# Another order of work on all five engines of an attention and feed-forward kernel, with four pieces of work on other engines

## The chip, the cores and the metric

The kernel runs on one core of one Trainium2 chip. The metric is the device time of one execution in microseconds. The core has five engines that each work through a queue of their own in order: TensorE (PE in the profile; PEld is its loading of weights), VectorE (DVE), ScalarE (ACT), GpSimd (POOL) and SyncE (SP), which here only issues DMA transfers.

## The reference

For each of 16 batch elements of 128 tokens by 256 features there is one attention layer with 32 heads of 8 features, whose keys and values come from a context of 128 tokens by 128 features, and one feed-forward layer of width 1024 with 4-bit rounding of weights and activations. Cut to what matters:

```python
q = layernorm(x) @ Wq ;  k, v = split(ctx @ Wkv)
q, k = rope(q, pos), rope(k, pos)
w = softmax(q k^T / sqrt(8))           # for each of 32 heads
x = x + (w v) @ Wout + bout
z = fake_quant(layernorm(x), s1, -8, 7)
h = z @ fake_quant(W1, max|W1|/7, -8, 7)^T + b1_q
h = fake_quant(relu(h), s2, 0, 15)
x = x + h @ fake_quant(W2, max|W2|/7, -8, 7)^T + b2_q
```

## The kernel before

One batch element b is the unit of work. Its way through the engines is:

- `project_qk` and `project_v` (TensorE), the rotation by `by_cosine` and `by_sine` (VectorE) and `rotate` (GpSimd), `transpose_rows` (TensorE). The result is split into a coarse part `T_hi` (`split_high`, ScalarE) and a rest `T_lo` (`split_low`, VectorE).
- SyncE stores both parts to the scratch tensor `scr` in DRAM and fetches them back in another layout, into `q_stack` and `k_stack`. There each head's 32 rows hold its features in both parts. The 128 partitions are four such row blocks, j = 0 to 3.
- The scores are computed twice, in four quarters u = 0 to 3. `scores_for_max(b, u)` writes `ps_max`, from bf16 halves, and VectorE's `maxima` reduces it. `transpose_maxima` and `copy_maxima` turn the maxima, and a DMA puts them into a spare row of `q_stack`. Then `scores_for_exp(b, u)` writes `ps_exp`, and ScalarE's `exponentials` reads it. `ps_max` and `ps_exp` exist once each, so quarter u waits until the reader of quarter u-1 is done.
- `weigh_values` (two halves), `copy_av`, `transpose_av`, `invert_sums` and `normalise`, `transpose_attn`, `copy_attnT`, `project_out`; then `residual`, `norm2_stats`, `norm2` (GpSimd), `round_x`, `clip_x`, `transpose_xq`, `copy_xqT`, `hidden` (two halves), `relu`, `clip_h`, `project_y`, `output`, `store`.

Which row blocks a quarter of scores uses is set by one line, the same in both score functions:

```python
j = 2 * (u % 2) + jj          # jj = 0, 1
rows = slice(32 * j, 32 * j + 32)
```

So quarters 0 and 2 use the row blocks 0 and 1, and quarters 1 and 3 use the row blocks 2 and 3.

The order on each engine is written out by hand as one loop over rounds s. `at(s - 3, work, u)` does the work for element b = s - 3 if there is one. The offset says how many rounds after the element's entry a step stands; the place in the list says what stands ahead of it in the round. The rounds of the different engines are counted apart. Elements enter one a round, so the last rounds hold only the late steps of the last elements.

Small matrix products share three PSUM banks, `ps_misc0` to `ps_misc2`. The table `BANK` says which piece uses which, and `claim` makes a piece wait until the reader of the piece ahead of it in the same bank is done.

Of the kernel before, what the change touches and what calls it, by code (L numbers as in the profile page):

```python
# [36 lines left out]
BANK = {"rows": 1, "y": 2, "xqT": 0, "h0": 0, "av": 1, "qk": 2, "attnT": 1, "h1": 1, "wo": 0, "w0": 1,  # L37
        "w1": 1, "v": 2, "mx": 0}
# [22 lines left out]
def xattn_ffn_kernel(nc, xin, pos, wq_d, wkv_d, wout_d, w1_d, w2_d, vecs_d, out_d):  # L61
    stack = ExitStack()
    with stack:
# [132 lines left out]
        wq_ready = sem("wq_ready")  # L196

# [51 lines left out]
        def _(sp):  # L249
# [82 lines left out]
            for s in range(BATCH + 8):  # L332
                if s == 5:
                    load_late()
                at(s - 4, fetch_keys, 1)
                at(s - 4, fetch_queries, 1)
                at(s - 5, place_maxima)
                if s == 4:
                    load_ffn(0)
                at(s - 3, store_q_hi)  # L340
                at(s - 8, store)
                at(s - 3, store_lo)
                at(s - 3, store_k_hi)
                if s == 4:
                    load_ffn(1)
                at(s, load_further)
                at(s - 3, fetch_queries, 0)
                at(s - 3, fetch_keys, 0)
            for r in range(2):
                sp.wait_ge(stored[r], 16 * BATCH // 2)  # L350

        @block.gpsimd
        def _(pool):
# [43 lines left out]

            pool.memset(ident[:, :], 0.0).then_inc(id_ready, 1)
# [7 lines left out]
            for s in range(BATCH + 5):  # L406
                at(s, norm)
                at(s - 3, residual_bias)
                at(s, rotate)
                at(s - 4, norm2)  # L410
                at(s - 5, output_bias)

        @block.scalar
        def _(act):
# [58 lines left out]
            for s in range(BATCH + 5):  # L473
                at(s - 3, exponentials, 1)
                at(s - 5, relu, 1)
                at(s - 3, exponentials, 2)
                at(s - 2, place_values)
                at(s - 3, exponentials, 3)
                at(s, split_high)
                at(s - 4, copy_xqT)  # L480
                at(s - 3, copy_av)
                at(s - 2, exponentials, 0)
                at(s - 4, relu, 0)
                at(s - 3, copy_attnT)

        @block.vector
        def _(dve):
# [45 lines left out]
            def fill_strips():  # L533


                dve.memset(v_strip[:, :, :, :, :], 0.0).then_inc(strips_ready, 1)
                dve.wait_ge(strips_ready, 1)
                for k in range(3):
                    dve.memset(v_strip[:, :, k::3, :, 9 * k + HD:9 * k + HD + 1], 1.0)
                dve.memset(v_strip[:, :, 7, :, 26:27], 1.0).then_inc(strips_ready, 1)  # L540

# [11 lines left out]
            def prepare_levels():  # L553
                dve.wait_ge(wmax_in_psum, 2)
                dve.tensor_copy(wmax_all[:, :], ps_misc[BANK["w1"]][:, 0:2]).then_inc(wmax_copied, 1)
                dve.wait_ge(wmax_copied, 1)
                link(dve.reciprocal(r_wmax[:, :], wmax_all[:, :]), wprep)
                link(dve.tensor_scalar(w_levels[:, :], r_wmax[:, :], QMAX, None, ALU.mult), wprep)
# [63 lines left out]

            def copy_maxima(b):
                need(dve, mx_in_psum, b + 1)
                if b >= 2:
                    dve.wait_ge(max_in[(b - 2) % STACKS], turn(b - 2, STACKS))
                dve.tensor_copy(mxT[:, b % 2, :], ps_misc[BANK["mx"]][0:HEADS, 0:128]).then_inc(mxT_ready, 1)
# [66 lines left out]
            for s in range(BATCH + 7):  # L694
                if s == 6:
                    quantise_weights(0)
                at(s - 7, output)
                at(s - 2, split_low)
                at(s - 3, maxima, 1)
                at(s - 5, invert_sums)  # L700
                if s == 4:
                    weight_maxima(1)
                at(s - 5, normalise)
                at(s, norm1_stats)
                at(s - 1, by_cosine)
                at(s - 3, maxima, 2)
                at(s - 1, by_sine)
                if s == 4:
                    spread_maxima()
                at(s - 5, residual)  # L710
                at(s - 3, maxima, 3)
                if s == 2:
                    fill_strips()
                at(s - 5, norm2_stats)
                if s == 5:
                    quantise_weights(1)
                if s == 4:
                    prepare_levels()
                if s == 3:
                    weight_maxima(0)  # L720
                at(s - 6, clip_h, 0)
                at(s - 6, clip_h, 1)
                at(s - 3, copy_maxima)
                if s == 4:
                    prepare_scales()
                    round_biases()
                at(s - 5, round_x)
                at(s - 5, clip_x)
                at(s - 2, maxima, 0)

        @block.tensor
        def _(pe):
# [164 lines left out]
            for s in range(BATCH + 6):  # L897
                at(s - 1, transpose_rows)
                at(s - 6, project_y)
                at(s - 5, transpose_xq)  # L900
                at(s - 4, weigh_values, 1)
                at(s - 2, scores_for_max, 1)
                at(s - 3, scores_for_exp, 0)
                at(s - 5, hidden, 0)
                at(s - 4, transpose_av)
                at(s, project_qk)
                at(s - 4, transpose_attn)
                at(s - 2, scores_for_max, 2)
                at(s - 3, scores_for_exp, 1)
                at(s - 5, hidden, 1)  # L910
                at(s - 4, project_out)
                if s == 3:
                    transpose_weight_maxima()
                at(s - 2, scores_for_max, 3)
                at(s - 3, scores_for_exp, 2)
                at(s - 3, weigh_values, 0)
                if s == 3:
                    spread_weight_maxima()
                at(s - 2, project_v)
                at(s - 2, transpose_maxima)  # L920
                at(s - 3, scores_for_exp, 3)
                at(s - 1, scores_for_max, 0)
# [47 lines left out]
```

## Time and profile before

| What | Value |
|---|---|
| Time, median of 3 runs | 241.31 us (241.07 to 246.26) |
| Time of the profiled execution | 240.79 us |
| Span of the profiled execution | 238.8 us |
| TensorE busy | 199.6 us (84%) |
| VectorE busy | 195.1 us (82%) |
| ScalarE busy | 149.3 us (63%) |
| GpSimd busy | 72.4 us (30%) |
| Mean granted TensorE clock | 0.897 of full |

The time is 2.0 us longer than the span. The span is what the trace covers. A share of busy time is a mean over the start, in which few elements are under way, the full middle, and the end.

### The profile page before, as it was taken

Reading aid. Unit: us, or ns where it says so; the run is one execution under the profiler, and the core shown is the slowest. Engines: PE = TensorE matmul, PEld = TensorE weight load, DVE = VectorE, ACT = ScalarE, POOL = GpSimd, SP = SyncE. Lnnn points to the kernel's source line nnn. Section 1 sums busy time; section 2 is a strip of 40 time slices with the busy share of each in tenths; the row PEclk is TensorE's granted clock in tenths of the full one; section 3 lists DMA queues with packets and bytes.
Section 4 is the critical chain, followed back from the end, with each engine's and each line's share of the span. In section 5 each row is a group of like instructions: output and inputs, shape, how many; then the busy total and the mean of one; then the engine's idle time right before and its main releaser. Section 6 shows DMA issues by size and latency. Waiting matters only on the chain.

```text
span 238.8 us, 7476 instructions
## 1 busy us (share of the span) xinstructions
PE 199.6 (84%) x2822; PEld 151.6 (63%) x2822; DVE 195.1 (82%) x394; ACT 149.3 (63%) x309; POOL 72.4 (30%) x121
## 2 busy tenths in 40 slices
PE   3453739799699999999999999899999987969653
PEld 2232416576478878878787878687877765757441
DVE  3555859979999999999999999999999979745241
ACT  4000004345487969787878788787979686878623
POOL 2432031402607162525334251607062303122030
PEclk9975555559899999999999999999999999999985
DMA  6358996519265848584856656685557362000000
GB/s 215 128 182 284 314 369 190 194 49 276 89 191 183 248 150 257 176 273 138 270 178 224 211 181 187 207 257 164 193 169 240 121 186 96 3 25 3 23 22 22
DMA packets 37234, 41.12 MB, mean 172 GB/s; under 512 B 2640, under 2 KB 34384, under 8 KB 36944
## 3 DMA queue, kind: packets, MB, share of 16 engines
q1 hardware_dynamic: 37056, 40.65, 53.0%
q8 instruction: 22, 0.36, 0.6%
q14 instruction: 12, 0.10, 0.2%
q10 hardware_dynamic: 144, 0.02, 0.0%
HBM read 25.19 MB, written 15.20 MB: 169 GB/s over the span
## 4 chain that ended last, share of the span: by engine, by line
PE 54%; issue 23%; DVE 8%; DMA 8%; POOL 4%; ACT 2%; ACTq 0%; POOLq 0%; DVEq 0%; SPq 0%
PE ps_misc L734 30%; PE ps_av L734 11%; PE ps_exp L734 7%; PE ps_max L734 6%; DMA q_stack<-scr 4%; DMA scr<-T_lo 2%; DVE mx L619 2%; POOL x_b L396 1%; DMA pos_sb<-in_fside_BxSx_dram 1%; POOL rot L375 1%; ACT h_i L464 1%; POOL x_b L382 1%; DVE wmax L544 1%; ACT T_hi L420 1%; DVE T_lo L611 1%
## 5 line engine op out<-in xcount | busy, mean ns | idle before, releaser
L619 DVE TENSOR_REDUCE mx<-ps_max 128x8 f32<-128x1024 f32 x64 | 77.8, 1216 | 8.4 <-PE ps_max L734 8.1
L436 ACT ACTIVATE expo<-ps_exp 128x1024 f32<-128x1024 f32 x64 | 65.8, 1028 | 15.6 <-PE ps_exp L734 14.1
L375 POOL TENSOR_TENSOR rot<-by_cos,by_sin 128x512 f32<-128x512 f32 x16 | 20.4, 1275 | 97.6 <-issue 92.2
L464 ACT ACTIVATE h_i<-ps_misc,b1q,relu_scale 128x128 int16<-128x128 f32 x128 | 47.8, 462 | 2.0 <-PE ps_misc L734 1.9
L734 PE MATMUL ps_exp<-q_stack,k_stack 32*128 32x128 f32 x512 | 44.8, 295 | 0.4 <-ACT expo L436 0.4
L734 PE MATMUL ps_max<-k_stack,q_stack 32*128 32x128 bf16 x512 | 28.0, 231 | 15.8 <-issue 8.2
L734 PEld LDWEIGHTS ps_exp<-q_stack,k_stack 32*128 32x128 f32 x512 | 35.5, 196 | 6.2 <-issue 5.1
L734 PE MATMUL ps_av<-expo,v_strip 128*32 128x128 f32 x1024 | 37.2, 289 | 0.1
L734 PEld LDWEIGHTS ps_max<-k_stack,q_stack 32*128 32x128 bf16 x512 | 16.3, 98 | 30.3 <-issue 15.4
L734 PEld LDWEIGHTS ps_av<-expo,v_strip 128*32 128x32 f32 x1024 | 27.7, 115 | 3.6 <-ACT expo L436 0.7
L734 PE MATMUL ps_misc<-wkv,x_in 128*128 128x256 f32 x64 | 24.1, 462 | 0.4 <-DMA wkv<-in_L_xattn_Wkv_dram 0.3
L420 ACT CAST T_hi<-ps_misc 128x512 fp32r<-128x512 f32 x16 | 9.3, 583 | 24.0 <-PE ps_misc L734 23.8
L388 POOL TENSOR_TENSOR rstd<-var,minus_half 128x1 f32<-128x1 f32 x16 | 10.3, 644 | 45.9 <-DVE var L661 45.9
L734 PE MATMUL ps_misc<-xqT,w1T 128*128 128x128 bf16 x256 | 20.6, 227 | 1.0 <-ACT xqT L454 0.6
L734 PE MATMUL ps_misc<-w2T,hq 128*128 128x256 bf16 x128 | 17.6, 281 | 3.2 <-DVE hq L680 3.2
L734 PE MATMUL ps_misc<-wq,x_in 128*128 128x256 f32 x64 | 20.0, 443 | 0.0
L734 PEld LDWEIGHTS ps_misc<-xqT,w1T 128*128 128x128 bf16 x256 | 15.2, 101 | 3.6 <-ACT attnT L448 0.7
L734 PE MATMUL ps_misc<-wout,attnT 128*128 128x256 f32 x64 | 17.4, 394 | 0.0
L430 ACT COPY v_strip<-ps_misc 128x96 f32<-128x96 f32 (+1 forms) x48 | 8.0, 244 | 14.9 <-PE ps_misc L734 14.9
L734 PEld LDWEIGHTS ps_misc<-wq,x_in 128*128 128x128 f32 x64 | 14.3, 226 | 2.9 <-DVE wq L530 0.4
L734 PEld LDWEIGHTS ps_misc<-w2T,hq 128*128 128x128 bf16 x128 | 12.3, 100 | 5.9 <-issue 3.5
L442 ACT COPY av<-ps_av 128x384 f32<-128x384 f32 x16 | 7.7, 478 | 12.4 <-PE ps_av L734 12.4
(93 smaller groups left out, 275.8 us busy)
## 6 DMA issues: line engine op xcount, KB each, us to landing
scr<-T_hi SPq DMA_DIRECT2D x32, 256.0 KB, 2.6
q_stack<-scr SPq DMA_DIRECT2D x32, 256.0 KB, 4.3
k_stack<-scr SPq DMA_DIRECT2D x32, 256.0 KB, 4.3
x_in<-in_xin_dram SPq DMA_DIRECT2D x16, 320.0 KB, 3.7
scr<-T_lo SPq DMA_DIRECT2D x16, 256.0 KB, 2.2
w<-in_L_ffn_W_dram SPq DMA_DIRECT2D x2, 1024.0 KB, 7.3
out_dram<-y SPq DMA_DIRECT2D x16, 128.0 KB, 1.7
scr<-pads SPq DMA_DIRECT2D x2, 256.0 KB, 4.3
```

Source lines behind the costliest of these rows:

```text
L375: pool.tensor_tensor(rot[:, b % 2, :], by_cos[:, :], by_sin[:, :], ALU.add).then_inc(rot_ready, 1)
L382: pool.tensor_tensor(x_b[:, b % 2, :], x_all[:, b, :], bout, ALU.add).then_inc(x_b_ready, 1)
L388: pool.tensor_tensor(rstd2[:, r, :], var2[:, r, :], minus_half[:, :], ALU.pow).then_inc(rstd2_ready, 1)
L396: pool.tensor_tensor(x2_b[:, r, :], x2[:, r, :], b2q[:, :], ALU.add).then_inc(x2_b_ready, 1)
L420: act.copy(T_hi[:, r, :, :].rearrange("p c e -> p (c e)"), ps_misc[BANK["rows"]][:, :]).then_inc(hi_ready, 1)
L430: ins = act.copy(v_strip[:, s, k::3, :, 9 * k:9 * k + HD], src[:, k::3, :, :])
L436: act.activation(expo[:, b % 2, u, :], ps_exp[:, :], ACT.Exp, scale=SCALE).then_inc(exp_done, 1)
L442: act.copy(av[:, r, :], ps_av[:, 0:384]).then_inc(av_copied, 1)
L464: ins = act.activation(h_i[:, r, f, :], ps_misc[BANK[("h0", "h1")[half]]][:, 128 * c:128 * c + 128], ACT.Relu, bias=b1q[:, f:f + 1], scale ...
L544: dve.tensor_reduce(out=wmax[:, n:n + 1], in_=w_flat[n], axis=AX.X, op=ALU.max, apply_absolute_value=True).then_inc(wmax_ready, 1)
L619: dve.tensor_reduce(out=out[:, 2 * (u % 2):2 * (u % 2) + 2, 4 * (u // 2):4 * (u // 2) + 4], in_=ps_max[:, :].rearrange("p (j g k) -> p j g ...
L734: return pe.matmul(out, lhsT, rhs, start=start, stop=stop, skip_group_check=True, **kw)
```

## The change

The loops of all five engines are written in another order and with other offsets. The loop of TensorE has BATCH + 8 rounds where it had BATCH + 6, that of VectorE BATCH + 10 (was BATCH + 7), that of SyncE BATCH + 11 (was BATCH + 8), that of GpSimd BATCH + 9 and that of ScalarE BATCH + 7 (both were BATCH + 5). The banks are shared out anew. Four pieces of work change their engine: the copy of the transposed maxima (`copy_maxima`) and the rounding of the two weight tensors (the first half of `quantise_weights`, now `round_weights`) go from VectorE to ScalarE, and `fill_strips` goes from VectorE to GpSimd, ahead of its loop. The clipping of the weights stays on VectorE as `clip_weights`.

```diff
-BANK = {"rows": 1, "y": 2, "xqT": 0, "h0": 0, "av": 1, "qk": 2, "attnT": 1, "h1": 1, "wo": 0, "w0": 1,
-        "w1": 1, "v": 2, "mx": 0}
+BANK = {"w0": 0, "wo": 0, "h1": 1, "w1": 2, "attnT": 2, "qk": 0, "v": 0, "rows": 1, "xqT": 2, "y": 0,
+        "mx": 0, "h0": 2, "av": 1}
...
+            def fill_strips():
+                pool.memset(v_strip[:, :, :, :, :], 0.0).then_inc(strips_ready, 1)
...
+            def round_weights(n):
+                act.wait_ge(levels_ready, 1)
+                act.activation(w_i[n][:, :], w_flat[n], ACT.Copy, scale=w_levels[:, n:n + 1]).then_inc(w_rounded[n], 1)
+
+            def copy_maxima(b):
+                need(act, mx_in_psum, b + 1)
+                if b >= 2:
+                    act.wait_ge(max_in[(b - 2) % STACKS], turn(b - 2, STACKS))
+                act.copy(mxT[:, b % 2, :], ps_misc[BANK["mx"]][0:HEADS, 0:128]).then_inc(mxT_ready, 1)
...
-            def quantise_weights(n):
-                link(dve.tensor_scalar(w_i[n][:, :], w_flat[n], w_levels[:, n:n + 1], None, ALU.mult), wprep)
+            def clip_weights(n):
+                dve.wait_ge(w_rounded[n], 1)
                 dve.tensor_scalar(w_q[n], w_i[n][:, :], QMIN, QMAX, ALU.max, ALU.min).then_inc(wq_ready, 1)
...
             column_means()
-            for s in range(BATCH + 6):
...
+            for s in range(BATCH + 8):
+                if s == 5:
+                    transpose_weight_maxima()
+                at(s - 7, project_out)
+                at(s - 2, scores_for_max, 1)
+                at(s - 4, scores_for_exp, 3)
+                at(s - 8, hidden, 1)
+                if s == 5:
+                    spread_weight_maxima()
+                at(s - 6, transpose_attn)
+                at(s, project_qk)
+                at(s - 4, weigh_values, 0)
+                at(s - 3, scores_for_exp, 0)
+                at(s - 2, scores_for_max, 2)
...
```

On TensorE the full rounds show it best. First the scores. `ps_exp` rows are a quarter of `scores_for_exp`, `ps_max` rows a quarter of `scores_for_max`; `wout` is `project_out`, `xqT,w1T` is `hidden`, `ident` with a tile is that tile's transpose, `wkv` and `wq` are `project_qk`. In a full round before, from `transpose_attn` on, with the quarters max 2, exp 1, then max 3, exp 2:

```order
L734 MATMUL ps_misc1<-ident,attn 128x128 x2
L734 MATMUL ps_max<-k_stack,q_stack 128x128 x8
L734 MATMUL ps_exp<-q_stack,k_stack 128x128 x8
L734 MATMUL ps_misc1<-xqT,w1T 128x128 x8
L734 MATMUL ps_misc0<-wout,attnT 128x256 x2
L734 MATMUL ps_max<-k_stack,q_stack 128x128 x8
L734 MATMUL ps_exp<-q_stack,k_stack 128x128 x8
L734 MATMUL ps_av<-expo,v_strip 32x128 x16
L734 MATMUL ps_misc2<-wkv,x_in 128x256
```

In a full round now, from `project_out` on, with the quarters max 1, exp 3, then exp 0, max 2:

```order
L743 MATMUL ps_misc0<-wout,attnT 128x256 x2
L743 MATMUL ps_max<-k_stack,q_stack 128x128 x8
L743 MATMUL ps_exp<-q_stack,k_stack 128x128 x8
L743 MATMUL ps_misc1<-xqT,w1T 128x128 x8
L743 MATMUL ps_misc2<-ident,attn 128x128 x2
L743 MATMUL ps_misc0<-wkv,x_in 128x256
L743 MATMUL ps_misc0<-wq,x_in 128x256 x2
L743 MATMUL ps_av<-expo,v_strip 32x128 x16
L743 MATMUL ps_exp<-q_stack,k_stack 128x128 x8
L743 MATMUL ps_max<-k_stack,q_stack 128x128 x8
```

Each `ps_max` row still stands beside a `ps_exp` row, but beside another quarter. The four neighbours of a round were (max 1, exp 0), (max 2, exp 1), (max 3, exp 2) and (exp 3, max 0). They are now (max 1, exp 3), (exp 0, max 2), (exp 1, max 3) and (exp 2, max 0).

Next the start of TensorE's queue, after the projection of elements 0 and 1. Before, the rows of element 1 (`ident,rot`) stand behind the first maxima scores of element 0:

```order
L734 MATMUL ps_misc1<-ident,rot 128x128 x4
L734 MATMUL ps_misc2<-wkv,x_in 128x256
L734 MATMUL ps_misc2<-wq,x_in 128x256 x2
L734 MATMUL ps_max<-k_stack,q_stack 128x128 x8
L734 MATMUL ps_misc1<-ident,rot 128x128 x4
L734 MATMUL ps_max<-k_stack,q_stack 128x128 x8
L734 MATMUL ps_misc2<-wkv,x_in 128x256
```

Now they stand ahead of them:

```order
L743 MATMUL ps_misc1<-ident,rot 128x128 x4
L743 MATMUL ps_misc0<-wkv,x_in 128x256
L743 MATMUL ps_misc0<-wq,x_in 128x256 x2
L743 MATMUL ps_misc0<-wkv,x_in 128x256
L743 MATMUL ps_misc1<-ident,rot 128x128 x4
L743 MATMUL ps_max<-k_stack,q_stack 128x128 x16
L743 MATMUL ps_misc0<-wkv,x_in 128x256
```

The rotated rows of element b moved from the round after `project_qk` into the same round, and its first maxima scores stayed in the round after, so that a round now lies between the two.

Last the end of TensorE's queue. Before, from the last but one `project_out` on, the last two elements' exponential scores and weighted values still stand between the steps of the feed-forward layer:

```order
L734 MATMUL ps_misc0<-wout,attnT 128x256 x2
L734 MATMUL ps_exp<-q_stack,k_stack 128x128 x8
L734 MATMUL ps_av<-expo,v_strip 32x128 x16
L734 MATMUL ps_exp<-q_stack,k_stack 128x128 x8
L734 MATMUL ps_misc2<-w2T,hq 128x256 x8
L734 MATMUL ps_misc0<-ident_bf,xq 128x128 x2
L734 MATMUL ps_av<-expo,v_strip 32x128 x16
L734 MATMUL ps_misc0<-xqT,w1T 128x128 x8
L734 MATMUL ps_misc1<-ident,av 128x128 x3
L734 MATMUL ps_misc1<-ident,attn 128x128 x2
L734 MATMUL ps_misc1<-xqT,w1T 128x128 x8
L734 MATMUL ps_misc0<-wout,attnT 128x256 x2
```

Now, from the `project_out` of element 13 on, nothing else is left for the last three elements:

```order
L743 MATMUL ps_misc0<-wout,attnT 128x256 x2
L743 MATMUL ps_misc1<-xqT,w1T 128x128 x8
L743 MATMUL ps_misc2<-ident,attn 128x128 x2
L743 MATMUL ps_misc2<-ident_bf,xq 128x128 x2
L743 MATMUL ps_misc0<-w2T,hq 128x256 x8
L743 MATMUL ps_misc2<-xqT,w1T 128x128 x8
L743 MATMUL ps_misc0<-wout,attnT 128x256 x2
L743 MATMUL ps_misc1<-xqT,w1T 128x128 x8
L743 MATMUL ps_misc2<-ident,attn 128x128 x2
L743 MATMUL ps_misc2<-ident_bf,xq 128x128 x2
L743 MATMUL ps_misc0<-w2T,hq 128x256 x8
```

Behind the last quarter of exponential scores there were 13 rows, and there are 26 now: `project_out`, `transpose_xq` and `hidden` of elements 13, 14 and 15 each have a round of their own behind it.

## Rows read from the trace of the kernel before

**Rows 1.** The page: busy time, TensorE's granted clock, the chain that ended last.

```profile
PE 199.6 (84%) x2822; PEld 151.6 (63%) x2822; DVE 195.1 (82%) x394; ACT 149.3 (63%) x309; POOL 72.4 (30%) x121
...
PEclk9975555559899999999999999999999999999985
...
PE 54%; issue 23%; DVE 8%; DMA 8%; POOL 4%; ACT 2%; ACTq 0%; POOLq 0%; DVEq 0%; SPq 0%
```

**Rows 2.** Windows: two full rounds; length, busy PE, PEld, DVE, ACT, POOL, then PEclk, DMA.

```profile
68.88:79.89 11.01, 11.01 (x176) 8.84 (x177) 10.76 (x23) 8.65 (x20) 4.40 (x7) 1.00 0.67 212
...
91.25:102.20 10.95, 10.95 (x177) 8.55 (x177) 10.70 (x23) 9.04 (x21) 4.39 (x7) 1.00 0.70 218
```

**Rows 3.** Timeline of TensorE at 2.4 GHz, scores issued together: start, length, operation.

```profile
166.87 0.23 PE L734 MATMUL ps_max<-k_stack,q_stack 32*128 32x128 bf16 x2
166.90 0.33 PE L734 MATMUL ps_exp<-q_stack,k_stack 32*128 32x128 f32 x2
...
167.49 0.62 PE L734 MATMUL ps_misc<-xqT,w1T 128*128 128x128 bf16 x8
```

**Rows 4.** The same view, scores that did not run together.

```profile
73.67 0.66 PE L734 MATMUL ps_exp<-q_stack,k_stack 32*128 32x128 f32 x8
74.26 0.41 PE L734 MATMUL ps_max<-k_stack,q_stack 32*128 32x128 bf16 x8
74.59 0.66 PE L734 MATMUL ps_misc<-ident,rot 128*128 128x128 f32 x4
```

**Rows 5.** The chain that ended last, in order of time: the trip through DRAM.

```profile
24.69 2.96 DMA scr<-T_lo
27.71 6.83 DMA q_stack<-scr
```

**Rows 6.** Timeline of TensorE: a fourth quarter's exponential scores, then the last element.

```profile
96.01 0.55 PE L734 MATMUL ps_exp<-q_stack,k_stack 32*128 32x128 f32 x6
...
218.66 0.66 PE L734 MATMUL ps_exp<-q_stack,k_stack 32*128 32x128 f32 x8 [0.35 <-ACT expo L436]
...
225.12 1.08 PE L734 MATMUL ps_misc<-wout,attnT 128*128 128x256 f32 x4
...
229.88 0.27 PE L734 MATMUL ps_misc<-ident_bf,xq 128*128 128x128 bf16 x2 [0.90 <-DVE xq L673]
230.70 1.87 PE L734 MATMUL ps_misc<-xqT,w1T 128*128 128x128 bf16 x16 [0.55 <-ACT xqT L454]
```

**Rows 7.** Timeline of VectorE: what follows the last output projection, and the end.

```profile
226.24 0.42 DVE L650 TENSOR_TENSOR x<-ps_misc,x_b 128x256 f32<-128x256 f32 x1 [2.60 <-PE ps_misc L734]
...
236.11 0.48 DVE L687 SCALAR_TENSOR_TENSOR y<-ps_misc,h_scale,x_b 128x256 f32<-128x256 f32 x1 [1.13 <-PE ps_misc L734]
```

**Rows 8.** Groups by line and shape: count, busy us, mean ns, idle time before.

```profile
L619 DVE TENSOR_REDUCE mx<-ps_max 128x8 f32<-128x1024 f32 x64 | 77.8, 1216 | 8.4 <-PE ps_max L734 8.1 <-issue 0.2
L436 ACT ACTIVATE expo<-ps_exp 128x1024 f32<-128x1024 f32 x64 | 65.8, 1028 | 15.6 <-PE ps_exp L734 14.1
...
L734 PE MATMUL ps_misc<-xqT,w1T 128*128 128x128 bf16 x256 | 20.6, 227 | 1.0 <-ACT xqT L454 0.6 <-ACT attnT L448 0.5
...
L734 PE MATMUL ps_misc<-wq,x_in 128*128 128x256 f32 x64 | 20.0, 443 | 0.0
L734 PE MATMUL ps_misc<-w2T,hq 128*128 128x256 bf16 x128 | 17.6, 281 | 3.2 <-DVE hq L680 3.2
L734 PE MATMUL ps_misc<-wout,attnT 128*128 128x256 f32 x64 | 17.4, 394 | 0.0
...
L627 DVE CAST mxT<-ps_misc 32x128 fp32r<-32x128 f32 x16 | 4.4, 272 | 0.7 <-PE ps_misc L734 0.7
L365 POOL TENSOR_SCALAR var<-mv 128x1 f32<-128x1 f32 x16 | 4.2, 261 | 5.6 <-DVE mv L589 5.6
...
L561 DVE TENSOR_SCALAR w_i<-w,w_levels 128x2048 int16<-128x2048 f32 x2 | 2.6, 1278 | 0.0
...
L403 POOL MEMSET pads<- 128x256 f32 x1 | 0.3, 311 | 0.0
```

More of the change, by code:

```diff
@@ L405, in _ @@
             pool.wait_ge(id_ready, 3)
-            for s in range(BATCH + 5):
+            fill_strips()
+            for s in range(BATCH + 9):
                 at(s, norm)
[L408 to L411, printed above, removed]
+                at(s - 8, norm2)
+                at(s - 9, output_bias)
+                at(s - 1, rotate)
+                at(s - 6, residual_bias)
         @block.scalar
@@ L693, in _ @@
             spread_tables()
[L694 to L724, printed above, removed]
+            for s in range(BATCH + 10):
+                at(s - 9, residual)
+                if s == 9:
+                    clip_weights(1)
+                at(s - 9, norm2_stats)
+                at(s - 4, maxima, 1)
+                if s == 8:
@@ new lines, in _ @@
+                at(s, norm1_stats)
+                at(s - 4, maxima, 3)
+                at(s - 10, output)
+                at(s - 2, split_low)
+                at(s - 3, maxima, 0)
+                if s == 4:
+                    weight_maxima(0)
+                if s == 6:
+                    spread_maxima()
+                at(s - 6, invert_sums)
+                if s == 6:
+                    prepare_levels()
+                at(s - 6, normalise)
+                if s == 5:
+                    weight_maxima(1)
@@ L896, in _ @@
             column_means()
-            for s in range(BATCH + 6):
-                at(s - 1, transpose_rows)
-                at(s - 6, project_y)
-                at(s - 5, transpose_xq)
-                at(s - 4, weigh_values, 1)
-                at(s - 2, scores_for_max, 1)
-                at(s - 3, scores_for_exp, 0)
-                at(s - 5, hidden, 0)
-                at(s - 4, transpose_av)
[L906 to L922, printed above, removed]
+            for s in range(BATCH + 8):
+                if s == 5:
+                    transpose_weight_maxima()
[3 more added lines that the diff above has]
+                at(s - 8, hidden, 1)
+                if s == 5:
+                    spread_weight_maxima()
[4 more added lines that the diff above has]
+                at(s - 2, scores_for_max, 2)
+                at(s - 4, weigh_values, 1)
+                at(s - 1, project_v)
+                at(s - 3, scores_for_exp, 1)
+                at(s - 2, scores_for_max, 3)
+                at(s, transpose_rows)
+                at(s - 7, transpose_xq)
+                at(s - 8, project_y)
+                at(s - 3, scores_for_exp, 2)
+                at(s - 1, scores_for_max, 0)
+                at(s - 2, transpose_maxima)
+                at(s - 7, hidden, 0)
+                at(s - 4, transpose_av)
 _INS = ['xin', 'fside_BxSx2_0', 'L0_xattn_Wq', 'L0_xattn_Wkv', 'L0_xattn_Wout', 'L0_ffn_W1', 'L0_ffn_W2', 'vecs']
```

74 lines of the change are left out of this document (39 added, 35 removed).

## Prediction

> **What bounds the kernel now.** I read the page first: TensorE is busy for 84% of the span and VectorE for 82%, and more than half of the chain that ended last is TensorE's own work [rows 1]. The strip of the granted clock gives the three stages: a start up to about 54 us, mostly at 1.2 GHz; a full middle at 2.4 GHz; an end. Then windows of two full rounds, from one `transpose_attn` to the next. They last 11.01 and 10.95 us; in them TensorE has no idle time that the view can show and VectorE is busy for 10.76 and 10.70 [rows 2]. So in the middle TensorE sets the pace, with VectorE 0.25 us behind. Whatever lengthens TensorE's round is paid every round; what only relieves VectorE is worth little. As a milestone I use the fourth quarter of the exponential scores, exp(b, 3): it starts at 96.01 us for element 4 and at 218.66 for element 15 [rows 6], which is 122.65 / 11 = 11.15 us per element, 0.2 more than TensorE's work. After the last one the kernel needs 238.8 - 218.66 = 20.1 us.
>
> **The score pairs.** This is the largest term. A quarter for the maxima and a quarter for the exponentials, issued one behind the other, took 166.87 to 167.49 = 0.62 us [rows 3], and the first exponential product began 0.03 us after the first of the maxima. Alone, an exponential quarter took 73.67 to 74.26 = 0.59, and a maxima quarter 74.26 to 74.59 = 0.33 [rows 4]. So in a pair the maxima quarter is all but free: 0.62 against 0.92. Every such pair before joins quarters on different row blocks: (max 1, exp 0) is blocks 2, 3 beside 0, 1, and so on. After the change all four pairs join quarters of the same parity, which means the same row blocks: (max 1, exp 3), (exp 0, max 2), (exp 1, max 3), (exp 2, max 0). No row before shows such a pair, so its price is bounded: 0.62 if nothing changes, 0.92 if the two just follow each other. I take 0.92, because exponential quarters show what happens within a block: eight products on two blocks took 0.59, and adding eight on the other two blocks added only 0.03, so it is the sequence within a block that costs. That is 4 x 0.30 = 1.20 us per round: 10.95 + 1.20 = **12.15 us** for a full round.
>
> The Trainium skill (TensorE: Matmul & The Clock Gate, Part 3, "The mechanism") says that a load of weights overlaps products in flight only when the row group differs; the trace agrees where it can, with 0.62 for a pair on different blocks, and by that rule the sum stays as it is. The same page (Part 2, "Step-by-step") also lets the load run ahead when it goes to the background weight buffer; by that the pair would cost less than 0.92, and this is the first rival below.
>
> **The other three engines in a full round.** VectorE loses `copy_maxima`, 272 ns [rows 8], and needs about 10.5 us of the 12.15. ScalarE gains it: 9.0 [rows 2] plus about 0.3. Neither is the bound any more. I followed the banks and the single `ps_max` and `ps_exp` through a round of the new order: a maxima quarter needs 1216 ns on VectorE [rows 8] and about 0.3 us of signalling, an exponential quarter 1028 ns on ScalarE and as much; the shortest distances between quarters on TensorE are about 2 us. `copy_maxima` now stands ahead of exp 2 on ScalarE and waits for `transpose_maxima`, which TensorE issues behind exp 2 and max 0; exp 2 is delayed by about 1 us, behind which exp 3 (2.5 us later) is still in time. So full rounds cost 12.15 and no more.
>
> **Work moved off VectorE once.** `fill_strips`: at 311 ns for 256 elements per partition [rows 8] GpSimd needs at most 12 x 0.311 = 3.7 us for 3072, and it sat idle for 5.6 us ahead of its first `var` [rows 8]. Hidden; if it were not, it costs at most 1 to 2 us there. VectorE did this while it waited for the first scores, so nothing is gained either. Rounding the weights: 2 x 1278 ns leave VectorE, 2 x about 2.06 us (twice 1028 for 1024 elements) enter ScalarE, between two exponential quarters. The levels now come from a chain TensorE, VectorE, TensorE, VectorE in TensorE's round 5. I count 1.3 us there. Before, the same work held TensorE for some 2 us, so this is no loss, included below.
>
> **The start.** Before, `T_lo` of element 1 is stored at 24.69 us and its trip through DRAM (2.96, then 6.83) [rows 5] stands within one round, between the transposed rows and the first maxima scores. Now a round lies between them, and the rows of element 1 no longer queue behind the maxima of element 0. Carried forward by hand with the old durations, `T_lo` of element 1 is ready 4 us earlier, but the four maxima quarters and the projections then take turns, with TensorE at 1.2 GHz as before, and exp(0, 3) starts at about 47 (48.5 before). TensorE's round 4 begins at 46.7. Rounds 4 to 6 lack `hidden`, `project_y`, `project_out` and small transposes: 20.6/16 + 17.6/16 + 17.4/16 = 3.5 [rows 8] (records of `hidden` overlap a little, which about pays for the small transposes), 12.15 - 3.5 = 8.65 at 2.4 GHz. Round 4 I put at 12.8 (half of it at 1.2 GHz, 1.5 of waits, because without `project_y` exp 2 comes too soon behind exp 1, and without `project_out` max 1 too soon behind max 0); round 5 at 11.5 with the weights, round 6 at 10.4, round 7 at 11.2. So round 8 begins at 92.6 and **exp(4, 3) at 94.0**, 2 us earlier than before. Bounds: 86 with no waits, 100 with as many again.
>
> **The middle.** Rounds 8 to 15: 8 x 12.15 = 97.2, to 191.2. Rounds 16 to 18 lack more and more steps of the front (`project_qk`, `transpose_rows`, `project_v`, the maxima): I get 10.3, 9.4 and 8.3. exp(15, 3) starts at 219.2, against 218.66 before.
>
> **The end.** Before, `project_out` of elements 13 and 14 were done beside the scores of element 15. Now TensorE does them in rounds 20 to 22, one after another, with nothing else to do. Each is a chain: from `project_out` to `transpose_xq` 229.88 - 225.12 = 4.76 us, through VectorE and GpSimd [rows 6, 7]; then 0.2 for that transpose, 1.0 for `project_y`, 0.5 for a half of `hidden`; 6.5 in all, and TensorE works for 3.5 of them. The next `project_out` stands behind it in the queue. So: the rest of round 19, 5.3; rounds 20 and 21, 13.0; round 22 up to `hidden` 6.0; and from `hidden` of the last element to the end 238.8 - 230.70 = 8.1 [rows 6]. Together **32.4 us where it was 20.1**. Bounds: 5 and 9 us a round in place of 6.5, so 28 to 40.
>
> **The sum.** 219.2 + 32.4 = 251.6 us of span. Against 238.8: start -2.0; eight full rounds 8 x (12.15 - 11.15) = +8.0; rounds 16 to 18, 28.0 - 33.5 = -5.5; end +12.3; together +12.8. The profiled execution took 2.0 more than its span, and its 240.79 is 0.5 under the median of 241.31, so I forecast **254.1 us**.
>
> **Rivals.** (1) The pairs are still free or half free. The products would overlap although they share blocks. For it: within a quarter, each of the four turns on a block takes 0.59 / 4 = 0.15 us, and some of that may be loading that another product can hide. Against it: the 0.59 and 0.33 add up when apart. Price: about 55 pairs, 0.30 each, is 16.5 us: 254.1 - 16.5 = 237.6 if free, 246 if half. (2) On the other side, the start. The trip through DRAM held TensorE in every early round, and now it does not. If TensorE runs rounds 4 to 7 on its work alone, with the pairs free too (7.45 instead of 8.65 a round), exp(4, 3) comes at 82 to 83; then 8 x 10.95 + 25.9 + 32.4 gives 228 to 229 of span, 231 in time. It decides itself at round 4: only if exp(4, 3) starts ahead of about 88 can the kernel be faster by over 2%. Against it: `ps_max` and `ps_exp` exist once, and VectorE and ScalarE need 1.5 us and 1.4 us between quarters whatever the order. (3) The clock falls in the end. It went back to 1.2 GHz at about 231 before, after TensorE had worked little; rounds 20 to 22 are half empty. At 1.2 GHz `project_out`, `project_y` and `hidden` add about 2.5 us a round: 254.1 + 7.5 = 261.6. The same price would come from a start that is 6 us later.
>
> **How the numbers follow.** The forecast's case (248 to 258) gets 0.62; half-free pairs (241 to 248) 0.12; free pairs (235 to 241) 0.12; the clock or a later start (258 to 266) 0.10; the fast start 0.04. The range 241 to 262 leaves out most of free pairs, the fast start and the top of the slow case, two in ten. 2% is about what a measurement of this kernel can tell from no change: 236.5 to 246.1. Above it lie the forecast, the slow case and a part of half-free pairs, 0.77; within it 0.18; below it 0.05.
>
> **What would show it.** In the profile of the changed kernel: the distance from a `ps_max` quarter through its `ps_exp` neighbour near 0.9 us and not 0.62; full rounds near 12.15 us with TensorE busy throughout and VectorE idle for over 1 us in each; exp(4, 3) near 94 and exp(15, 3) near 219; behind it 32 us with three `project_out` 6.5 us apart. The prediction is wrong if pairs stay at 0.62, if full rounds wait for VectorE or ScalarE (a wait of `scores_for_max` for `maxima` in every round), or if the last `project_out` follows exp(15, 3) within 15 us.

## The result and the profile after

The changed kernel took 248.99 us (median of 4 runs, 247.4 to 250.68), the kernel before it 241.78 us beside it (4 runs, 241.07 to 246.26). The ratio is 1.031, with an interval of 1.025 to 1.037: the change makes the kernel slower. Here and below, ratios leave out runs that are over 1.5% longer than the shortest of their kernel, while medians count every run. The profiled execution took 247.4 us with a span of 245.6, which is 6.8 more than before.

The page of the changed kernel: busy time, TensorE's granted clock, and the chain that ended last, to be laid beside [rows 1]. A digit of PEclk is the clock granted to TensorE in one of 40 slices, in tenths of full speed.

```profile
PE 208.4 (85%) x2822; PEld 161.0 (66%) x2822; DVE 190.0 (77%) x371; ACT 152.2 (62%) x327; POOL 74.7 (30%) x126
...
PEclk9855757589958999999999999999999999997797
...
PE 51%; issue 23%; DMA 10%; DVE 6%; POOL 6%; ACT 2%; SPq 1%; ACTq 0%; POOLq 0%; DVEq 0%
```

TensorE has the same 2822 matmuls and is busy for 8.8 us more. The work is the same, so it got dearer where it stands. VectorE is 5 us less busy, and that bought nothing.

Windows of the changed kernel: a full round from `transpose_attn` to `transpose_attn`, and 2 us ahead of the full rounds (length, busy PE, PEld, DVE, ACT, POOL, then PEclk and DMA).

```profile
94.19:105.64 11.45, 11.45 (x180) 9.22 (x177) 10.79 (x22) 8.89 (x21) 4.42 (x7) 1.00 0.64 191
70.00:72.00 2.00, 2.00 (x14) 1.79 (x13) 1.90 (x6) 2.00 (x2) 0.00 (x0) 0.50 0.83 202
```

A full round is 11.45 us long where it was 11.01 and 10.95 [rows 2]. TensorE has no idle time in it, and VectorE is idle for 0.66. The second row is a loss that I hadn't looked for: at 2.4 GHz TensorE had just had three short waits, and then its clock was 1.2 GHz (granted 0.50) while TensorE, VectorE and ScalarE were full.

Timeline of TensorE after (start, length, operation, idle before), at two pairs of quarters in one full round and then the fourth quarter of element 15.

```profile
96.81 0.66 PE L743 MATMUL ps_exp<-q_stack,k_stack 32*128 32x128 f32 x8
97.32 0.40 PE L743 MATMUL ps_max<-k_stack,q_stack 32*128 32x128 bf16 x8
97.65 1.08 PE L743 MATMUL ps_av<-expo,v_strip 128*32 128x128 f32 x32
...
104.39 0.40 PE L743 MATMUL ps_max<-k_stack,q_stack 32*128 32x128 bf16 x8
104.61 0.64 PE L743 MATMUL ps_exp<-q_stack,k_stack 32*128 32x128 f32 x8
105.18 0.51 PE L743 MATMUL ps_misc<-xqT,w1T 128*128 128x128 bf16 x6
...
211.47 0.66 PE L743 MATMUL ps_exp<-q_stack,k_stack 32*128 32x128 f32 x8
...
216.99 1.09 PE L743 MATMUL ps_misc<-wout,attnT 128*128 128x256 f32 x4
...
221.75 0.27 PE L743 MATMUL ps_misc<-ident_bf,xq 128*128 128x128 bf16 x2 [2.77 <-DVE xq L685]
...
224.18 1.75 PE L743 MATMUL ps_misc<-wout,attnT 128*128 128x256 f32 x4
...
229.43 0.37 PE L743 MATMUL ps_misc<-ident_bf,xq 128*128 128x128 bf16 x2 [2.82 <-DVE xq L685]
...
232.16 1.18 PE L743 MATMUL ps_misc<-wout,attnT 128*128 128x256 f32 x4
...
237.00 0.27 PE L743 MATMUL ps_misc<-ident_bf,xq 128*128 128x128 bf16 x2 [3.22 <-DVE xq L685]
```

The two quarters of a pair now stand one behind the other in the trace, and no longer begin together as in [rows 3]. From start to start the pair takes 96.81 to 97.65 = 0.84 us with the exponentials first, and 104.39 to 105.18 = 0.79 with the maxima first, against 0.62. In the eight full rounds from 96.81 us on all 32 pairs take 0.78 to 0.84. The last three `project_out` begin at 216.99, 224.18 and 232.16. In each of these rounds TensorE waits about 3 us for `xq`, the end of the chain from the output projection through VectorE and GpSimd. Before there was one such round behind the scores [rows 6].

In three pieces, with exp(4, 3) at 93.16 and exp(15, 3) at 211.47, against the milestones of before [rows 6]: the start is 96.01 - 93.16 = 2.85 us shorter. The middle is 118.31 where it was 122.65, 4.3 shorter. What follows the last score is 245.6 - 211.47 = 34.1 where it was 20.1, 14.0 longer. The sum is +6.8. The middle is shorter in spite of longer full rounds. From exp(4, 3) to exp(12, 3) it takes 91.6 us where it took 89.5; from there to exp(15, 3) 26.7 where it took 33.2, since its last rounds have lost the feed-forward steps of the late elements. Those steps reappear in the end.

The kernel before didn't reach the 10.95 us of its best round in every round: the mean of those eight is 11.19. The pair of exp 3 and max 0 is the part of the round that varies. Timeline of TensorE before:

```profile
129.33 0.66 PE L734 MATMUL ps_exp<-q_stack,k_stack 32*128 32x128 f32 x8
130.47 0.40 PE L734 MATMUL ps_max<-k_stack,q_stack 32*128 32x128 bf16 x8 [0.48 <-issue]
```

In the nine full rounds from 96 to 186 us this fourth pair takes from 0.60 to 1.65 us, 1.04 in the mean, though it is on different row blocks; the other three take 0.61 or 0.62 each time. The view names no releaser. An estimate from the views of SyncE and of the tile puts it down to the trip through DRAM: the fetch of `k_stack` was issued at 125.74 and the median from issue to landing is 4.6, which is 130.3. In the new order a round lies between that trip and max 0.

### The profile page after: what moved, and what is told of

Its sections match the earlier page's. It is cut to its first block, busy times and chain, and to the rows that moved or that the text cites. A ratio compares the mean times of both kernels' runs of the same rounds, so it can differ in the third digit from the quotient of the medians.

```text
span 245.6 us, 7474 instructions
## 1 busy us (share of the span) xinstructions
PE 208.4 (85%) x2822; PEld 161.0 (66%) x2822; DVE 190.0 (77%) x371; ACT 152.2 (62%) x327; POOL 74.7 (30%) x126
## 4 chain that ended last, share of the span: by engine, by line
PE 51%; issue 23%; DMA 10%; DVE 6%; POOL 6%; ACT 2%; SPq 1%; ACTq 0%; POOLq 0%; DVEq 0%
PE ps_misc L743 27%; PE ps_exp L743 10%; PE ps_av L743 9%; PE ps_max L743 5%; DMA scr<-T_hi 4%; DMA w<-in_L_ffn_W_dram 4%; POOL x_b L384 2%; POOL x_b L398 2%; DVE mx L637 2%; DMA pos_sb<-in_fside_BxSx_dram 1%; DMA k_stack<-scr 1%; POOL rot L377 1%; ACT h_i L486 1%; ACT expo L448 1%; DVE by_sin L622 1%
## 5 line engine op out<-in xcount | busy, mean ns | idle before, releaser
L448 ACT ACTIVATE expo<-ps_exp 128x1024 f32<-128x1024 f32 x64 | 65.1, 1018 | 29.6 <-PE ps_exp L743 28.2
L743 PE MATMUL ps_av<-expo,v_strip 128*32 128x128 f32 x1024 | 35.2, 280 | 0.0
L390 POOL TENSOR_TENSOR rstd<-var,minus_half 128x1 f32<-128x1 f32 x16 | 8.9, 558 | 84.9 <-DVE var L673 84.9
L743 PEld LDWEIGHTS ps_av<-expo,v_strip 128*32 128x32 f32 x1024 | 26.7, 112 | 6.9 <-issue 5.0
L743 PE MATMUL ps_misc<-wkv,x_in 128*128 128x256 f32 x64 | 24.8, 474 | 3.5 <-DVE by_sin L622 3.3
L743 PE MATMUL ps_misc<-wq,x_in 128*128 128x256 f32 x64 | 21.0, 460 | 0.5 <-DVE wq L557 0.5
L743 PEld LDWEIGHTS ps_misc<-xqT,w1T 128*128 128x128 bf16 x256 | 16.7, 102 | 2.1 <-DVE attn L654 0.4
L743 PEld LDWEIGHTS ps_misc<-wkv,x_in 128*128 128x128 f32 x64 | 11.1, 217 | 8.4 <-DVE by_sin L622 4.3
L613 DVE TENSOR_TENSOR by_cos<-ps_misc,tabs 128x512 f32<-128x512 f32 x16 | 11.0, 690 | 7.0 <-PE ps_misc L743 6.0
L699 DVE SCALAR_TENSOR_TENSOR y<-ps_misc,h_scale,x_b 128x256 f32<-128x256 f32 x16 | 7.7, 483 | 11.1 <-PE ps_misc L743 11.1
```

What stands on the lines that cost most here:

```text
L390: pool.tensor_tensor(rstd2[:, r, :], var2[:, r, :], minus_half[:, :], ALU.pow).then_inc(rstd2_ready, 1)
L613: dve.tensor_tensor(by_cos[:, :].rearrange("p (c h d) -> p c h d", c=2, d=HD), ps_heads, bcast(tabs[:, b, :, 0:8], 2, HEADS), ALU.mult).th ...
L699: dve.scalar_tensor_tensor(out=y[:, r, :], in0=ps_misc[BANK["y"]][:, 0:DIM], scalar=h_scale[:, 1:2], in1=x2_b[:, r, :], op0=ALU.mult, op1= ...
L743: return pe.matmul(out, lhsT, rhs, start=start, stop=stop, skip_group_check=True, **kw)
```

## The experiments

Two causes were on record, the shared row blocks and the lengthened end. The first four kernels were made to take them apart, and to put them into the kernel before. All four ran on one chip and the later ones on others, each group beside the kernel before (241.26, 242.88 and 242.69 us), so across groups the ratios are surer than differences in us.

**Row blocks apart.** In the changed kernel only, the maxima quarters change parity, in the scores and in where `maxima` stores them. Each maxima quarter then stands beside an exponential quarter on the other two row blocks, in the same order of instructions.

```diff
-                out=out[:, 2 * (u % 2):2 * (u % 2) + 2, ...]
+                out=out[:, 2 * ((u + 1) % 2):2 * ((u + 1) % 2) + 2, ...]
...
-                        j = 2 * (u % 2) + jj
+                        j = 2 * ((u + 1) % 2) + jj
```

> The changed kernel with one thing undone: a quarter of the maxima scores now takes the other two row blocks (and the reduction writes the other columns), so that each of the four score pairs of a round joins quarters on different row blocks again, as in the kernel before. Order, banks and moved work stay as changed. Theory (pairs on shared blocks cost 0.79 to 0.84 us instead of 0.62): the round falls from 11.45 us to about 10.6, unless another engine takes over; with some 14 rounds under load this gives 8 to 11 us, so 237 to 240 us. Rival (the blocks do not matter and the round of 11.45 is due to waits of the new order): pairs keep 0.8 us and the time stays at 247 to 250.

It took 240.49 us (10 runs), ratio 0.994 to before (0.990 to 0.998), 8.5 us less than the changed kernel. Its full round:

```profile
101.25:112.00 10.75, 10.75 (x179) 8.59 (x177) 10.58 (x22) 8.71 (x21) 4.46 (x7) 1.00 0.72 216
```

Timeline of TensorE in that round, at one pair (start, length, operation).

```profile
103.88 0.33 PE L743 MATMUL ps_exp<-q_stack,k_stack 32*128 32x128 f32 x2
103.91 0.34 PE L743 MATMUL ps_max<-k_stack,q_stack 32*128 32x128 bf16 x6
...
104.47 1.08 PE L743 MATMUL ps_av<-expo,v_strip 128*32 128x128 f32 x32
```

In three of the four pairs the quarters begin together again, and this one is down to 104.47 - 103.88 = 0.59 us. The fourth, exp 2 and max 0, runs together only in part and takes 109.02 - 108.27 = 0.75; in other rounds it takes 0.64 to 0.75:

```profile
108.27 0.66 PE L743 MATMUL ps_exp<-q_stack,k_stack 32*128 32x128 f32 x8
108.68 0.41 PE L743 MATMUL ps_max<-k_stack,q_stack 32*128 32x128 bf16 x8
109.02 0.29 PE L743 MATMUL ps_misc<-ident,mx 128*32 128x128 f32 x1
```

The four pairs of this round take 2.54 us against 3.30 in the changed kernel's, which covers the 0.70 by which the round is shorter than 11.45. exp(4, 3) comes at 89.44, 3.7 us earlier than in the changed kernel, and exp(15, 3) at 201.78, 9.7 earlier. The end is as long as in the changed kernel, 236.5 - 201.78 = 34.7, so in the trace the row blocks leave the end alone.

**Row blocks shared.** The same edit in the kernel before, where it brings the pairs onto the same blocks.

> The kernel before with the same edit the other way round: its four score pairs now join quarters on the same row blocks, and nothing else is changed. Theory (shared blocks cost about 0.2 us a pair): the round grows from 10.95 to 11.75 us, 0.8 x 14 = 8 to 11 us more, so 249 to 253 us. Rival (the blocks do not matter): 241 to 242 us.

It took 245.87 us (4 runs), ratio 1.020 (1.012 to 1.028): slower than before, though by less than the 249 to 253 that I expected. The span is 242.4, 3.6 more than before. A full round and a pair in it:

```profile
104.05:115.45 11.40, 11.40 (x178) 9.35 (x178) 10.99 (x23) 8.97 (x21) 4.39 (x7) 1.00 0.58 182
```

```profile
104.37 0.40 PE L734 MATMUL ps_max<-k_stack,q_stack 32*128 32x128 bf16 x8
104.58 0.64 PE L734 MATMUL ps_exp<-q_stack,k_stack 32*128 32x128 f32 x8
105.15 0.62 PE L734 MATMUL ps_misc<-xqT,w1T 128*128 128x128 bf16 x8
```

The pair takes 0.78 us here too, so sharing is what makes it dear and not the new order. The round grew from 10.95 to 11.40, but the mean from exp(4, 3) to exp(15, 3) only from 11.15 to (222.62 - 97.76) / 11 = 11.35. The reason is the fourth pair, exp 3 and max 0. The three pairs with the maxima first went from 0.62 to 0.78 each, +0.5 us a round, but the fourth often stood apart already: its mean over nine full rounds was 1.04 before and is 0.89 here, so there was little overlap left for the shared blocks to take.

**One round less.** In the changed kernel everything from `transpose_attn` on stands one round earlier on all engines, and the weights' clipping, the scales and the late load with it. Only the offsets are touched.

```diff
-            for s in range(BATCH + 8):
+            for s in range(BATCH + 7):
...
-                at(s - 7, project_out)
+                at(s - 6, project_out)
```

> The changed kernel with everything from the transpose of the normalised attention on done one round earlier on all engines; the places within a round, the banks and the moved work stay. Theory (the end costs a round of its own for each late element, 6.5 to 8 us): one such round goes away, so 6 to 8 us less, 240 to 243 us, and the full rounds stay at 11.45. Rival 1 (the end is set by the clock, or by the chain of the last element alone): 247 to 250. Rival 2 (a round less of slack makes the full rounds wait for the normalisation): full rounds over 12 us, time 250 or more.

It took 242.75 us (10 runs), ratio 1.008 (1.003 to 1.012), 6.2 us less than the changed kernel. Rounds last 11.45 us as before the edit, exp(15, 3) comes at 213.67, and 240.6 - 213.67 = 26.9 us follow in place of 34.1. Two `project_out` are left behind the round of the last score, at 219.19 and 225.50. The end is 7.2 shorter; 2.2 of it went into the start, where exp(4, 3) now comes at 95.31 and not at 93.16. I put that down to the late steps entering its rounds sooner; it isn't shown.

**Both edits together.** Both mended, in the changed kernel.

> The changed kernel with both edits: different row blocks in each score pair, and the late steps one round earlier. If the two causes are separate, their gains add: 8 to 11 and 6 to 8 us off 249, so 230 to 235 us. If the start or VectorE is the bound without the shared blocks, less than the sum: 236 to 240.

It took 234.06 us (4 runs), ratio 0.972 (0.966 to 0.979). The two gains, 8.5 and 6.2, add up to 14.7, and both together gave 14.9. On this one chip, with the other edit in place each time, the row blocks are worth 242.75 - 234.06 = 8.7 us and the round 240.49 - 234.06 = 6.4. Rounds last 10.75, and 27.0 us follow the last score. The new order without its two costs is better than the old one.

**The strips later.** `fill_strips` moves behind the first three `norm` on GpSimd, out of the start.

```diff
-            fill_strips()
             for s in range(BATCH + 9):
                 at(s, norm)
+                if s == 2:
+                    fill_strips()
```

> The changed kernel with the filling of the value strips still on GpSimd, but in its round 2, where the trace shows 4 us of idle time, instead of ahead of its loop. Theory (GpSimd's fill from 1.93 to 4.59 us held VectorE's first copy, 0.98 us long instead of 0.18, and with it the whole start): the first copy takes 0.18 us again, every milestone of the start comes 0.9 us earlier, and the time falls by about 1 us, to 248. Rival (the longer first copy has to do with the late arrival of its input): the first copy stays at 0.98, no gain.

I made it because of these rows of the changed kernel. First VectorE at the start, then GpSimd (two calls of the same timeline):

```profile
3.65 0.98 DVE L525 COPY ang<-pos_sb 128x32 f32<-128x32 f32 x1 [2.67 <-DMA pos_sb<-in_fside_BxSx_dram]
3.74 0.91 DVE L526 TENSOR_SCALAR ang<-pos_sb 128x32 f32<-128x32 f32 x1
...
1.93 2.66 POOL L403 MEMSET v_strip<- 128x3072 f32 x1
...
8.48 0.24 POOL L367 TENSOR_SCALAR var<-mv 128x1 f32<-128x1 f32 x1 [3.54 <-DVE mv L607]
```

A copy of 32 elements took 0.98 us and ended at 4.63, 0.04 behind the end of the fill. GpSimd itself still waited 3.54 us ahead of its first `var`. With the strips filled later, in this kernel and in the one with all three edits alike, the same copy reads

```profile
3.61 0.18 DVE L526 COPY ang<-pos_sb 128x32 f32<-128x32 f32 x1 [2.63 <-DMA pos_sb<-in_fside_BxSx_dram]
```

So 0.8 us at the start is shown, and the first `var` of GpSimd comes at 7.78 and not at 8.48. The time was 248.73 us (4 runs, 245.88 to 259.3), ratio 1.019 (1.009 to 1.030) against 1.031 (1.025 to 1.037) for the changed kernel. The intervals overlap, so a gain in the total isn't shown. The profiled execution was the longest of the four; only its first microseconds are read here.

**The copy of the maxima back on VectorE**, behind `maxima(s - 3, 0)`; ScalarE loses it.

```diff
-                at(s - 2, copy_maxima)          # ScalarE
...
                 at(s - 3, maxima, 0)
+                at(s - 4, copy_maxima)          # VectorE
```

> The changed kernel with the copy of the transposed maxima back on VectorE, behind the reduction of the next element's first quarter. Theory (the forecast's: VectorE is not the bound, so where the copy runs is worth nothing by itself; but on VectorE it now stands behind a reduction of 1.22 us, and project_out waits for it through its bank): full rounds 0.3 to 0.5 us longer than 11.45, 4 to 6 us more in all, 252 to 254. Rival (the copy is hidden on either engine): 248 to 250.

It took 263.95 us (5 runs, 258.97 to 264.76). The ratio on record, 1.092 (1.084 to 1.099), rests on the three longest runs; the two shortest, 258.97 and 262.28, give 1.076. So the price is 12 us by the shortest runs and 15 by the medians and the profiled executions (262.28 against 247.4). My expectation, 4 to 6 us more, missed by at least a factor of two. A round lasts 123.91 to 136.30 = 12.39. TensorE, then VectorE, at its edge:

```profile
134.58 0.28 PE L743 MATMUL ps_misc<-ident,mx 128*32 128x128 f32 x1
...
136.30 0.92 PE L743 MATMUL ps_misc<-wout,attnT 128*128 128x256 f32 x3 [0.66 <-DVE mxT L638]
```

```profile
134.85 1.22 DVE L630 TENSOR_REDUCE mx<-ps_max 128x8 f32<-128x1024 f32 x1
135.98 0.27 DVE L638 CAST mxT<-ps_misc 32x128 fp32r<-32x128 f32 x1
```

The transposed maxima lie in bank 0, and `project_out` uses bank 0 next. The copy can't run before the reduction ahead of it on VectorE is done, at 136.07, and `project_out` waits for that copy in twelve rounds, 7.9 us in all. The wait is 0.66 of the 0.94 us by which the round is longer than 11.45. The rest lies in the products on either side of it, which overlap less: from the start of the transposes ahead of `project_out` to `project_out` it is 1.16 us, the wait included, where it was 0.33, and from there to the next score 1.07 where it was 0.96, together 0.94. In the profiled executions 8.2 us lie between exp(4, 3) and exp(15, 3), and exp(4, 3) itself comes 7.3 later, at 100.43. That is half of the price. The strip of the granted clock shows 1.2 and 2.4 GHz by turns there, with a slice of 0.5 as late as 85 to 91 us, so a part of it may be clock; I haven't split it up. The price holds for this place in VectorE's list; other places weren't tried.

**The rounding of the weights back on VectorE**, ahead of their clipping.

```diff
-                dve.wait_ge(w_rounded[n], 1)
+                link(dve.tensor_scalar(w_i[n][:, :], w_flat[n], w_levels[:, n:n + 1], None, ALU.mult), wprep)
                 dve.tensor_scalar(w_q[n], w_i[n][:, :], QMIN, QMAX, ALU.max, ALU.min).then_inc(wq_ready, 1)
```

> The changed kernel with the rounding of both weight tensors back on VectorE, in its rounds 7 and 9 just ahead of the clipping. Theory (done once, beside other work): within 1 us of the changed kernel, 248 to 250. Rival (VectorE is full in rounds 7 and 9, TensorE waits there): 2 to 3 us more, 251 to 252.

It took 249.14 us (4 runs), ratio 1.027 (1.018 to 1.036). Beside the changed kernel's 248.99 and 1.031 no difference can be measured.

**All three edits.** Row blocks apart, one round less, and the strips later.

> The changed kernel with three edits: score pairs on different row blocks, late steps one round earlier, value strips filled in GpSimd's round 2. If the third gain adds to the other two (14.9 us together), about 1 us less than the 234.1 us of those two: 233. If the first step is hidden there: 234.

It took 232.04 us (4 runs), ratio 0.959 (0.952 to 0.965): 4.1% faster than the kernel before, and faster than the changed one. Against the kernel with two edits it is 2.0 us less, but on another chip, and the intervals (0.952 to 0.965 and 0.966 to 0.979) all but touch, so how much of that is the strips stays open.

**One round more.** The kernel before, with everything from `transpose_attn` on one round later on all engines: the lengthened end alone, without the new order.

```diff
-            for s in range(BATCH + 6):
+            for s in range(BATCH + 7):
```

> The kernel before with everything from the transpose of the normalised attention on done one round later on all engines, and nothing else changed. Theory (each late element that is left over at the end costs a round of its own): full rounds stay near 11 us, the time behind the last exponential scores grows from 20 to 26 or 27 us, 241.3 + 6 = 247 to 248 us, the changed kernel's loss in the end shown in the kernel before. Rival (before loses time by a wait of the transpose for VectorE, 4.2 us in four places, that a later round takes away, and the chain at the end is as long in any case): 238 to 242.

It took 248.82 us (4 runs), ratio 1.026 (1.012 to 1.041), 6.1 more than the 242.69 of the kernel before beside it. Rounds last 11.0 us, exp(15, 3) came 2.9 us earlier, at 215.79, and 245.9 - 215.79 = 30.1 us followed, where I had expected 26 to 27. Timeline of TensorE from its second last `project_out`:

```profile
222.33 1.08 PE L734 MATMUL ps_misc<-wout,attnT 128*128 128x256 f32 x4
...
227.50 1.01 PE L734 MATMUL ps_misc<-xqT,w1T 128*128 128x128 bf16 x8 [0.55 <-ACT xqT L454]
...
231.20 2.02 PE L734 MATMUL ps_misc<-wout,attnT 128*128 128x256 f32 x4
```

The chain round took 8.87 us, with TensorE busy for 4.65 of it. At 222.33 `project_out` took 1.08 us, at 231.20 2.02: the clock had fallen to 1.2 GHz in between. So a round of depth cost this end 10.0 us, more than the chain of waits at the full clock, and 2.9 of them were won back ahead of it.

## Why the prediction was right and wrong

The direction and both large causes were right, and the start came out as forecast in part by luck. 254.1 was forecast and 248.99 measured, inside the range. In the span the forecast was 251.6 and the profile has 245.6; the terms were off as follows.

**The score pairs: the mis-sized term.** The mechanism was right, as the two kernels with changed parity show from both sides. The step that failed is "4 x 0.30 = 1.20 us per round: 10.95 + 1.20 = 12.15 us". A pair costs 0.79 to 0.84 in place of the 0.92 that I took, which is 0.17 to 0.22 more than 0.62; four pairs come to about 0.8 and not 1.2. And the base was too high: the new order alone, with blocks apart, has a round of 10.75 and not 10.95. The statement that every pair before was nearly free was wrong too: the two quarters of [rows 4], read there as quarters alone, are the fourth pair, exp 3 and max 0, on different blocks and still 0.92 long. So 10.95 was the best round before and not the usual 11.19, and the new order won back what that pair lost. A full round is 11.45, not 12.15. Eight of them make 8 x 0.70 = 5.6 us, of the 6.0 by which the span was over-forecast; the start (-0.8), rounds 16 to 18 (-1.3) and the end (+1.7) nearly cancel. I had reasoned that "it is the sequence within a block that costs", and chose the upper end of 0.62 to 0.92 outright. The trace shows something in between: on the same blocks a pair is still about 0.1 us shorter than 0.92. The Trainium skill (TensorE: Matmul & The Clock Gate, Part 3, "The mechanism") has weight loads overlap only where the row group differs. The trace agrees with its direction, 0.59 against 0.84 for the same two quarters, but the 0.92 that two separate quarters would give wasn't reached.

Between half-free pairs (246) and the forecast (254.1) the measured time lies nearly in the middle, so the first rival was half right as to size. With a price bounded only from both sides, its upper end was the wrong single value: the middle, 0.77, was nearer to what came.

**VectorE and ScalarE: right.** No full round waits for either, and in the window after VectorE has 0.66 us to spare. What I had not seen is what the new place of `copy_maxima` prevents. I read it as 272 ns of relief for an engine that doesn't bind. Put back on VectorE behind a reduction, in the place tried, it held `project_out` through the shared bank, 0.94 us a round, and the kernel took 12 to 15 us more. The price of a moved operation was read from its duration, when it lay in who waits behind it.

**Work moved once: half right.** The rounding costs nothing that can be measured on either engine, as the kernel with it back shows. "Hidden" for `fill_strips` was true on GpSimd's queue and wrong for the chip: it held VectorE's first copy for 0.8 us, at a time when nothing else covered it. I had asked only whether GpSimd was idle.

**The start: right, in part by luck.** exp(0, 3) came at 47.16 against 47, exp(4, 3) at 93.16 against 94.0. The rounds between were not as forecast: they took 11.9, 10.8, 12.8 and 10.5 us where I had 12.8, 11.5, 10.4 and 11.2. Three were shorter and the third 2.4 longer. In it TensorE's clock, forecast at 2.4 GHz, was at 1.2 from 69.5 to about 75 us:

```profile
69.48 0.61 PE L743 MATMUL ps_max<-k_stack,q_stack 32*128 32x128 bf16 x8 [0.59 <-DVE mx L637]
69.85 1.10 PE L743 MATMUL ps_exp<-q_stack,k_stack 32*128 32x128 f32 x8
...
82.69 0.64 PE L743 MATMUL ps_exp<-q_stack,k_stack 32*128 32x128 f32 x8
```

The fast start, the second rival, didn't come.

**The middle.** Forecast 219.2 - 94.0 = 125.2, measured 118.3. Beside the 5.6 of the full rounds, 1.3 lie in rounds 16 to 18. I haven't split them up; they have score pairs too, whose price was too high.

**The end: right, slightly short.** 32.4 forecast and 34.1 measured. The chain rounds took 224.18 - 216.99 = 7.2 and 232.16 - 224.18 = 8.0 in place of 6.5, and from the last `hidden` to the end 245.6 - 238.00 = 7.6 in place of 8.1. This is the third rival in part: a lower clock in the end, at well under the 2.5 us a round that it priced. Windows after, the two chain rounds (columns as above; the mean granted clock is the third number from the right):

```profile
216.99:224.18 7.19, 4.37 (x34) 3.31 (x33) 4.41 (x11) 3.50 (x10) 1.97 (x3) 0.86 0.05 18
224.18:232.16 7.98, 5.16 (x35) 4.06 (x33) 3.16 (x9) 3.64 (x10) 1.24 (x2) 0.71 0.05 17
```

TensorE was busy for 4.4 and 5.2 us, where I had reckoned with 3.5 at 2.4 GHz, and that is about the size by which the rounds are longer than 6.5. The depth of the loops is the cause of the end, shown twice: one round less in the changed kernel took 6.2 us off the time, one round more in the kernel before added 6.1.

Of the 7.2 us between the two kernels, the two causes explain more than all. With the blocks apart the changed order is at 240.49, even with the kernel before, and with the depth of one round taken back too it is 2.8% faster. The change bought a shorter start and a leaner order, and paid for both with the row blocks and the long end.

## What to carry to other kernels

When small products with few rows are issued side by side, write down the row blocks of each neighbouring pair before and after a reordering; here one line of parity was worth 8.5 us. Every round by which a late step is pushed back costs its whole chain of waits once more at the end, about 6 us of the time here, however well it hides in the full rounds. Of an operation that changes engines ask who waits behind it, through the bank it occupies and the port it uses, and not only how long it takes.

## What the hardware did that I had not expected

- A fill of 3072 elements per partition on GpSimd (1.93 to 4.59) stretched a VectorE copy of 32 elements from 0.18 to 0.98 us. The same shows in 13 of the 16 runs of `clip_x`, which makes `xq`. Timeline of the changed kernel in a full round, VectorE and then GpSimd, and its group by line (count, busy us, mean ns, idle before):

```profile
98.90 0.80 DVE L685 TENSOR_SCALAR xq<-xq_i 128x256 bf16<-128x256 int16 x1
...
98.88 0.73 POOL L384 TENSOR_TENSOR x_b<-x_in,vecs 128x256 f32<-128x256 f32 x1
...
L685 DVE TENSOR_SCALAR xq<-xq_i 128x256 bf16<-128x256 int16 x16 | 9.9, 622 | 0.2
```

  At 229.06, with GpSimd idle, it took 0.23. Its mean was 328 ns before and is 622 now, since in the full rounds `residual_bias` (the second row) has come to start just ahead of it. With the row blocks apart both still run side by side, but of the two `xq` starts first, and then takes 0.21. VectorE and GpSimd there:

```profile
105.91 0.21 DVE L685 TENSOR_SCALAR xq<-xq_i 128x256 bf16<-128x256 int16 x1
...
105.94 0.77 POOL L384 TENSOR_TENSOR x_b<-x_in,vecs 128x256 f32<-128x256 f32 x1
```

  So 0.02 us behind `residual_bias` or 0.03 ahead of it makes the difference between 0.80 and 0.21, though spans on GpSimd are rough. The Trainium skill (SBUF — State Buffer, "SBUF: two separate sides") calls the port pair that both engines share an exclusive lock, which whoever comes second waits out. The rows agree, in the order of starting too; no run was made to tell that from another cause.
- Two score quarters on the same row blocks still save about 0.1 us when issued together: 0.79 to 0.84 us, where a pair on different blocks whose quarters didn't run together took 0.59 + 0.33.
- TensorE's clock fell to 1.2 GHz ahead of the full rounds (granted 0.50 from 70 to 72 us), behind three waits of 0.29, 0.76 and 0.59 us between 66 and 69.5, and in part of the half-empty rounds of the end (0.86 and 0.71 in the mean). I hadn't put the first fall in the sum. That the waits caused it is a reading of one trace; no run tried it.
